# Cross-attention and a top-2 mixture of experts on one core: routing logits from folded weights, norms after the gather, a new lead-in and drain

## What is computed

```python
x = x + xattn(k=ctx, q=layernorm(x), v=ctx)     # 16 heads of 8, causal, out-projection Wo, bias bo
xf = layernorm(x).reshape(1792, 128)
logits = xf @ gate_w + gate_b                   # 8 experts
p, i = top_k(softmax(logits), 2); p = p / sum(p)
# each expert takes its first 280 tokens, in order of the tokens
out = relu(xin @ w1[e] + b1[e]) @ w2[e] + b2[e] # 128 -> 512 -> 128, per expert
x = x + (sum over the token's two experts of p * out)
```

## Time and profile before

| what | value |
|---|---|
| three runs | 191.65, 193.49, 194.66 us (median 193.49) |
| the profiled execution | 194.35 us, of which its span is 192.6 us |
| mean granted TensorE clock | 0.885 |
| busy share of the span: PE, PE weight loads, DVE, ACT, POOL | 83%, 57%, 58%, 45%, 47% |

### The profile page before, as it was taken

The page is one execution under the profiler, slowest core; times in us unless marked ns, Lnnn a source line. Parts: engine busy times, 40 slices in busy tenths (PEclk is TensorE's granted clock), DMA queues, the critical chain, the costliest instruction groups (busy, mean ns, idle before and its releaser), DMA issues.

```text
span 192.6 us, 4628 instructions
## 1 busy us (share of the span) xinstructions
PE 159.1 (83%) x1647; PEld 109.8 (57%) x1651; DVE 110.9 (58%) x395; ACT 87.3 (45%) x196; POOL 90.7 (47%) x152
## 2 busy tenths in 40 slices
PE   6588779999999999999999896965399999998000
PEld 2323537777777777767677543422179988886000
DVE  4666534668889888889886553200026554555064
ACT  3547595979797977884735101000123222330000
POOL 4345290014157765757577787761002644656300
PEclk9855766999999999999999999996859999999655
DMA  5910798995000000000100000003700110111666
GB/s 164 327 75 0 300 388 230 338 311 162 0 3 26 31 29 26 14 27 5 37 0 23 4 20 6 16 8 77 198 0 0 44 39 27 31 34 35 240 189 247
DMA packets 10109, 17.96 MB, mean 93 GB/s; under 512 B 1708, under 2 KB 5568, under 8 KB 9576
## 3 DMA queue, kind: packets, MB, share of 16 engines
q1 hardware_dynamic: 6992, 13.58, 21.4%
q0 software_dynamic: 1632, 2.27, 3.9%
q10 hardware_dynamic: 1464, 1.84, 3.0%
HBM read 11.00 MB, written 7.86 MB: 98 GB/s over the span
## 4 chain that ended last, share of the span: by engine, by line
PE 64%; DMA 8%; POOL 7%; issue 6%; ACT 6%; DVE 5%; ACTq 1%; POOLq 1%; DVEq 1%; SPq 0%
PE score_p L977 10%; PE bank L1005 8%; PE bank L1149 7%; PE bank L992 6%; PE score_p L946 5%; PE score_p L1133 5%; PE bank L1133 5%; POOL slots_d L405 3%; PE bank L905 3%; PE bank L938 3%; DMA chosen<-choice_d 3%; DMA xr<-slots_d 2%; PE bank L1022 2%; PE bank L918 2%; DMA choice_d<-rest_ow,rest_i 2%
## 5 line engine op out<-in xcount | busy, mean ns | idle before, releaser
L405 POOL DMA_INDIRECT slots_d<-rec,slot_i x32 | 32.3, 1008 | 13.9 <-issue 12.4
L911 PE MATMUL score_p<-warm 128*128 128x512 bf16 x91 | 24.9, 419 | 6.0 <-DMA slots_d<-rec,slot_i 3.8
L443 POOL DMA_INDIRECT choice_d<-ow,dst_i x16 | 16.0, 1000 | 29.3 <-DVE ow L871 26.4
L674 DVE TENSOR_REDUCE row_max<-score_p 128x16 f32<-128x912 f32 x16 | 17.7, 1104 | 10.6 <-PE score_p L977 10.6
L977 PE MATMUL score_p<-head_keys,queries 32*32 32x228 f32 (+1 forms) x384 | 22.1, 409 | 0.0
L550 ACT ACTIVATE probsT<-bank 128x512 f32<-128x512 f32 x32 | 18.2, 600 | 5.0 <-PE bank L992 4.9
L992 PE MATMUL bank<-ident,probs 128*128 128x128 f32 x128 | 19.6, 291 | 0.0
L911 PEld LDWEIGHTS score_p<-warm 128*128 128x128 bf16 x95 | 9.5, 106 | 16.9 <-DMA slots_d<-rec,slot_i 4.3
L677 DVE TENSOR_TENSOR probs<-score_p,row_max 128x912 f32<-128x912 f32 x16 | 17.7, 1109 | 1.6
L335 POOL TENSOR_TENSOR rs<-ve,minus_half 128x2 f32<-128x2 f32 x8 | 6.3, 791 | 24.8 <-DVE ve L653 21.2
L1005 PE MATMUL bank<-vals,probsT 128*64 128x18 f32 x512 | 17.8, 212 | 0.0
(11 more groups left out here) (130 smaller groups left out, 281.7 us busy)
## 6 DMA issues: line engine op xcount, KB each, us to landing
choice_d<-chosen SPq DMA_DIRECT2D x2, 1024.0 KB, 8.1
w_s<-w_in SPq DMA_DIRECT2D x1, 2048.0 KB, 8.9
slots_d<-zeros SPq DMA_DIRECT2D x1, 1242.0 KB, 4.4
xg<-slots_d SPq DMA_DIRECT2D x8, 138.0 KB, 4.1
chosen<-choice_d SPq DMA_DIRECT2D x1, 1024.0 KB, 5.0
xs<-x_in SPq DMA_DIRECT2D x1, 768.0 KB, 7.1
ctxT<-ctx_t_in SPq DMA_DIRECT2D x1, 768.0 KB, 8.4
b_s<-b_in SPq DMA_DIRECT2D x1, 512.0 KB, 9.0
```

Source lines behind the costliest of these rows:

```text
L405: gp.indirect_dma_start(out=slots_d, out_offset=bass.IndirectOffsetOnAxis(ap=slot_i[t % 2][:, k, p:p + 1], axis=0), in_=rec[t % RECS][:, p ...
L443: gp.indirect_dma_start(out=choice_d, out_offset=bass.IndirectOffsetOnAxis(ap=where, axis=0), in_=rows, in_offset=None, bounds_check=N_DST ...
L674: ve.reduce_max(row_max[:, p, :], heads, X).then_inc(max_d, 1)
L911: mm(bank[0], warm[:, 0:128], warm[:], start=True, stop=True)
```

## The change

1. **Logits.** A layer norm is linear but for its mean and its factor rs, so logits = rs * ((x + attention + bo) @ G) + gate_b with G = the gate weights less their column means. `centre_gate` makes G (`gate_c`) once on TensorE, `fold_gate` makes Wo @ G once and puts it beside Wo. `output` then multiplies `yT` by 136 columns in place of 128 and adds `xT` (x transposed, given by the host, bo added on GpSimd by `add_bo_T`) times G, 8 columns. `turn_moe`, `empty_moe` and `gate` go. VectorE copies the 16 raw logits out (`gates`) and multiplies by rs in `choose` (two instructions in place of one).
2. **Records.** `x2` now lies inside the record, which also holds mean and rs; `records` goes, and so do the three buffers with their waits. The rows are normalised after the gather: `normalise_slots(e)` and `normalise_rest`, two VectorE instructions of 128x128 for each expert and two for the rest, ahead of the transposes.
3. **Order.** The loop runs to step 7 only; what followed is written out. `choose` is for group g-2 in step g (behind `softmax(2g+1)`), `ranks` and `slots` for g-3 stand earlier in the step. Norm and projection run one group ahead in place of two. The last group's weights are made on VectorE (`weigh_last`).
4. **Lead-in.** The first keys go to a bank of their own, their first copy stands ahead of `empty_norm(0)`, the first queries are copied out on VectorE, 10 filler matmuls stand in the gaps of TensorE, `scores(1)` stands ahead of the wait for the mean, and the clearing of `chosen` on GpSimd comes later.
5. **Gather.** SP issues the load of half of `xr` right behind `xg[0]`; the transposes no longer wait for the third, small one.

```diff
-WARM_START, WARM_TURN, WARM_GATE, WARM_RANK = 11, (2, 4, 12), 2, (4, 6, 8)
-WARM_LAST, WARM_SCATTER, WARM_LANDING = 5, 28, 9
+WARM_LEAD = (3, 2, 2, 3)
+WARM_START = 11
+WARM_MIX, WARM_Y, WARM_CHOICE, WARM_SCATTER, WARM_LANDING = 2, 2, (3, 11), 30, 9
...
+            sp.dma_start(xT[:], x_t).then_inc(xT_in, 16)
...
+                if e == 0:
+                    sp.dma_start(xr[:, 1], by_expert[1]).then_inc(xr_in, 16)
...
             power1(0)
             power1(1)
-            gp.memset(chosen[:, 0], 0.0).then_inc(empties_done, 1)
             means()
...
+            t = GROUPS - 1
+            weigh(t - 2)
+            count(t - 2)
+            scatter(t - 2, 0, 3)
+            power2(t - 1)
+            scatter(t - 2, 3)
+            weigh(t - 1)
+            power2(t)
+            count(t - 1)
+            scatter(t - 1)
+            scatter(t)
...
-            empty_keys("k", 0, 0).then_inc(ring_ev, 1)
+            act.wait_ge(keys0_d, 1)
+            keys0 = probT_b[0][:, 0:2 * GP * S]
+            head_copy(0, 0, keys0)
             empty_norm(0)
-            act.wait_ge(bqs_done, 1)
-            empty_queries("q", 0).then_inc(ring_ev, 1)
+            for h in range(1, SH):
+                last = head_copy(0, h, keys0)
+            last.then_inc(keys0_ev, 1)
...
-            act.dma_start(xr[0:REST, STACKS], by_expert[STACKS - 1, STACK - 1]).then_inc(xr_in, 16)
+            act.dma_start(xr[:, 0], by_expert[0]).then_inc(xr_in, 16)
+            act.dma_start(xr[0:REST, STACKS], by_expert[STACKS - 1, STACK - 1]).then_inc(xr_last_in, 16)
...
-            def records(t):
...
             def choose(t):
...
+                dve.wait_ge(rs2_d, t + 1)
...
                 for p in range(GP):
+                    ve.scalar_tensor_tensor(logits[:, p, :], gates[:, p, :], rec[:, GP * t + p, RS:RS + 1],
+                                            gate_b[:, E * p:E * (p + 1)], mult, add).then_inc(logits_d, 1)
...
+            def normalise_slots(e):
+                dve.wait_ge(xg_in[e], 16)
+                for t in range(FULL):
+                    ve.tensor_scalar(xg[:, e, t, 0:D], xg[:, e, t, 0:D], xg[:, e, t, MEAN:MEAN + 1], xg[:, e, t, RS:RS + 1],
+                                     sub, mult).then_inc(xgn_d, 1)
...
             def expert(e, i):
+                if e + 1 < E:
+                    normalise_slots(e + 1)
...
             def output(t):
+
+                pe.wait_ge(xboT_d, t + 1)
                 pe.wait_ge(ring_ev, filled("y", t))
                 to = take_post("wo", t)
...
+                    n = GP * t + p
+                    mm(to[:, WO * p:WO * (p + 1)], yT[:, 128 * p:128 * (p + 1)], wvo_s[:, D:D + WO], start=True, stop=False,
+                       skip_group_check=True)
+                    last = mm(to[:, WO * p + D:WO * (p + 1)], xT[:, 128 * n:128 * (n + 1)], gate_c[:], start=False, stop=True,
+                              skip_group_check=True)
...
+            keep_warm(WARM_LEAD[2], probT_b[1][:])
             project(1)
+            keep_warm(WARM_LEAD[3], probT_b[1][:])
+            scores(1)
             pe.wait_ge(mean_done, 1)
             tr(post("mean", 0)[:, 0:B], mean[:], ident[0:B, 0:B]).then_inc(post_d, 1)
-            scores(1)
-            values(0)
+            centre_gate()
             transpose_probs(0)
             transpose_probs(1)
-            norm(2)
-            project(2)
...
             def transpose_slots(e, i):
-                pe.wait_ge(xg_in[e], 16)
+                pe.wait_ge(xgn_d, FULL * (e + 1))
```

More of the change, by code:

```diff
@@ new lines, in statistics2, with choose @@
+            def statistics2(t):
+                dve.wait_ge(x2_d, t + 1)
+                hold(dve, passed["dve"])
+                tiles = slice(GP * t, GP * (t + 1))
+                stats(x2[:, tiles, :], stat2, rec[:, tiles, MEAN:RS + 1], stat2_d, mv2_d, GP * t)
+                wait(dve, rs2_d, t)
+                ve.tensor_scalar(ve2[:], rec[:, tiles, RS], 1e-5, None, add).then_inc(ve2_d, 1)
+            def choose(t):
+                tiles = slice(GP * t, GP * (t + 1))
+                dve.wait_ge(rs2_d, t + 1)
+                dve.wait_ge(post_read, posted("wo", t))
+                wait(dve, top_i_d, t)
@@ L784, in _ @@
             statistics1(1)
+            dve.wait_ge(ring_d, filled("q", 0))
+            ve.tensor_scalar(queries[0][:], ring("q", 0)[:, 0:GT], SCALE, bqs[:], mult, add).then_inc(ring_ev, 1)
+            shift1(1)
             keep(slice(GP, PAIRS), 2)
@@ L794, in _ @@
             statistics1(2)
+            softmax(1)
             shift1(2)
@@ new lines, in _ @@
+                if g >= 2:
+                    statistics2(g - 2)
+                softmax(GP * g + 1)
+                if g >= 2:
+                    choose(g - 2)
+                if 0 <= g + 3 < GROUPS:
+                    statistics1(g + 3)
+                divide(GP * (g - 1))
+            t = GROUPS - 1
+            divide(PAIRS - 3)
+            slots(t - 2)
+            divide(PAIRS - 2)
+            residual(t - 1)
+            statistics2(t - 1)
+            divide(PAIRS - 1)
+            choose(t - 1)
@@ new lines, in _, with normalise_rest @@
+            residual(t)
+            statistics2(t)
+            slots(t - 1)
+            choose(t)
+            weigh_last(t)
+            slots(t)
+            def normalise_slots(e):
[3 more added lines that the diff above has]
+                                     sub, mult).then_inc(xgn_d, 1)
+            def normalise_rest():
+                dve.wait_ge(xr_in, 16 * STACKS)
+                for k in range(STACKS):
+                    ve.tensor_scalar(xr[:, k, 0:D], xr[:, k, 0:D], xr[:, k, MEAN:MEAN + 1], xr[:, k, RS:RS + 1], sub, mult)\
+                        .then_inc(xrn_d, 1)
@@ L874, in expert @@
                     weigh_rest(2, slice(0, REST), 3)
+            normalise_slots(0)
+            normalise_rest()
             dve.wait_ge(wb_in, 32)
@@ L1097, in _ @@
                 transpose_probs(4 * g + 1)
+            t = GROUPS - 1
+            mix(PAIRS - 3)
+            ranks(t - 2)
+            mix(PAIRS - 2)
+            turn_y(t - 1)
+            transpose_probs(UNITS - 2)
+            transpose_probs(UNITS - 1)
+            output(t - 1)
+            mix(PAIRS - 1)
+            keep_warm(WARM_MIX)
+            turn_y(t)
+            keep_warm(WARM_Y)
+            output(t)
+            keep_warm(WARM_CHOICE[0])
+            ranks(t - 1)
+            keep_warm(WARM_CHOICE[1])
+            ranks(t)
             def transpose_slots(e, i):
-                pe.wait_ge(xg_in[e], 16)
+                pe.wait_ge(xgn_d, FULL * (e + 1))
                 wait(pe, xgT_ev, e - 1)
```

399 lines of the change are left out of this document (200 added, 199 removed).

## The result

The changed kernel took 180.31, 180.39, 184.67 and 184.69 us, median 182.53; the kernel before took 191.65 to 194.66, median 193.25, on the same chip. The forecast was 178.0 with a range of 173 to 184. The profiled execution of the changed kernel took 180.31 with a span of 178.6; that of before took 194.35 with a span of 192.6. So -14.0 between the two traces, where the forecast was -16.6.

What follows compares the result with a forecast made beforehand. TensorE was taken to bound the loop steps and experts, GpSimd to pace the drain. -9.7 - 0.8 - 2.5 - 2.3 - 1.8 + 0.5 = -16.6 gave 177.75 for an execution like the profiled one, forecast as 178.0, range 173 to 184.

Steps and rivals of the forecast that it cites:

- The lead-in: Stretch up to the heads of step 2: these start at 29.0 in place of 38.69, so -9.7 us.
- The rival with the fallen clock: Lead-in: the clock falls all the same and costs 4 us more, giving 182; chance 15%.
- the 0 that was taken: Lead-in: cost of GpSimd's clearing of `chosen` holding VectorE, taken as 0 of 0 to +1.8 us.
- The steps: Loop steps 2 to 6: 51.35 us in place of 52.15, so -0.8, bounds -1.2 and +2.4.
- near 10.35: Steps 3 to 6: VectorE's time per step after losing `records` and gaining a copy and a small instruction, taken as step time.
- TensorE's own 10.27: Loop steps: TensorE's time per full step, from 10.64, losing record transposes and gate and gaining two products.
- The rival named for this: Steps are VectorE's: the residual waits for `output`, 0.8 a step, making 11.1 a step and 181.5 us; chance 5%.
- The drain: Step 7's heads to the last record's landing, paced by GpSimd: 38.75 us in place of 41.2, so -2.5.
- The gather: Last record's landing to first w1 matmul: 5.3 us in place of 7.6, so -2.3.
- landed 3.2 us behind the records: Gather: both halves of `xr`, moved ahead in their queues, land 3.2 us after the records.
- The clock behind the gather: First expert: fillers and less idle time recover clock loss, -1.8 us of 0 to -2.6.
- Expert 1: Added normalisations on VectorE not hidden there, with `set_rest` in front: +0.5 us, range 0 to +1.

Runs made afterwards that it cites:

- run 1: Changed kernel without the ten filler matmuls of the lead-in: 180.68, 185.61, 186.01 and 186.04 us.
- run 3: Changed kernel without the two products of the input with the centred gate in each output stage: 179.4 us, one execution.
- run 4: Changed kernel with two normalisations of a record put back on VectorE behind choose in each step, into an unread tile: 184.18 us.
- run 10: Changed kernel with epsilon added to both variances on GpSimd, not VectorE; on another chip: 208.88 us, beside 211.09 to 215.69 for the kernel before.
- run 12: Changed kernel with the four edits of run 11, and epsilon on GpSimd up to group 5; another chip: median 202.07 us, kernel before 211.23.
- run 6: Changed kernel with group 6's power behind two scatters, not three, and set_rest inside expert 1: 181.95 us.
- run 5: Changed kernel with SyncE waiting for both halves of xr before loading xg 1 to 7: median 180.66 us, ratio 0.9423.
- run 7: Changed kernel with seven and two filler matmuls in the two holes of the gather: 178.63 us, one execution.
- run 9: Changed kernel with xr's second half issued ahead of xg[0]; another chip: 205.37 us, beside 211.09 to 215.69 for the kernel before.
- run 11: Changed kernel with the edits of run 6 and run 7 plus four fillers ahead of pair 2's scores; another chip: 198.83 to 203.11 us, ratio 0.939.

## Why the prediction was right, and where it was wrong

The forecast of 178.0 lies 2.3 below the shortest execution (180.31) and 4.5 below the median, within the range of 173 to 184.

**The lead-in (-9.7, came -9.8)** holds in place and size: heads of pair 2 at 18.95 (said 18.7), of step 2 at 28.88 (said 29.0), VectorE's small instruction behind the mask down from 1.32 to 0.20. But the reason given for the clock was the order, which "leaves no idle stretch over 1 us". It leaves one of 1.09, and without the ten fillers, which the prediction's working doesn't count, three of four executions were long and the profiled one lost 5.9 of the 9.8 (run 1). So that the term came out whole in the profiled execution is in part luck. The rival with the fallen clock, put at 15% and +4, happened in four of nine profiled executions with this lead-in (1.5 to 2.9 late), and two of the changed kernel's four executions were 4.4 longer for a reason that no trace shows.

The clearing of `chosen` (18.42 to 20.23) met VectorE's small instruction at 19.38, which took 0.87 and ended with it, against 0.17 otherwise. The prediction had named this from the Trainium skill, SBUF — State Buffer, section "The single rule", by which one of the two engines holds the shared ports for its whole instruction; this row agrees. The softmax behind it started 0.19 behind the end of its scores, where it is 0.11 otherwise, so the 0 that was taken stands within 0.1.

**The steps (-0.8, came +0.5).** Two terms failed. "9.95 for step 2" was 10.46: it was 10.10 before, when TensorE had no records to transpose and no gate in it to lose, and it gains the products (run 3 takes 0.34 off it). And "near 10.35" for steps 3 to 6 was 10.72, 10.70, 10.52 and 10.26. The 10.35 was VectorE's term, reckoned from less work than before, and that is where it went wrong: VectorE was busy for 9.65, 9.55 and 9.45 in steps 3 to 5, where it had been for 9.23, 9.50 and 8.88. The prediction counted on TensorE the norm and projection that the old lead-in had done ahead, and not the statistics that VectorE makes for them: six such instructions on `xs` lie in steps 3 to 5, where it was two. Runs 3 and 4 show that VectorE sets steps 3 to 5, where what is taken off TensorE brings nothing. TensorE's own 10.27 isn't borne out either: with VectorE relieved, step 3 stays at 10.48 (runs 10 and 12). The rival named for this had the right engine and the wrong price (0.8 a step through the wait for `output`; steps 3 to 5 came out 0.2 to 0.4 above 10.35), and 5% was too little for it.

**The drain (-2.5, came -3.1)** was GpSimd's, as said. The scatters of group 5 began to be paid for at 95.19, 13.65 behind the heads of step 7 (said 14.0), and from there to the last scatter's end it took 23.3 (said 23.6). What wasn't foreseen is the 0.67 us that GpSimd waits for the choice of group 6, whose power stands behind three scatters; run 6 took it out. The sign "a granted clock of 1.00 from about 5 us to the landing" failed here: it was 0.50 from 96 to 100 us. No run fills that hole, so what it costs isn't known.

**The gather (-2.3, came -1.4).** The step that failed is "landed 3.2 us behind the records": xr came 4.5 behind them. From issue to landing the half on SP's queue takes 4.08 now, and the load waited for before took 4.48; what was gained is mostly that the load the transposes wait for is issued 0.45 behind the landing and not 1.87, minus 0.6 for the normalising. Run 5 shows that the loads behind it in the queue aren't the reason; what is, stays open. The Trainium skill, DMA: Bandwidth & Descriptors, section "Issuing engines are not separate DMA queues", gives an issue on another queue no more than the time of the issue. This trace agrees in part, since 1.42 of the 1.82 by which `xr` landed earlier is time of issue. By the one issue (0.5) that the prediction drew from it the gather would have come to -0.5, as far from -1.4 on the one side as the forecast on the other.

**The clock behind the gather (-1.8, came -0.95)** was mis-sized: the first expert took 5.70 in place of 6.65. Thirty fillers ahead of the landing and nine right at it don't help against the 4 us behind them (122 to 126) in which TensorE works for 1.04; "no such hole behind it" is what failed. Nine more fillers in those 4 us gave another 1.68 (run 7): together the 2.6 that was the far end of the term. **Expert 1 (+0.5)** came out at +0.64, and run 6 showed that `set_rest` is its cause.

So the direction and the place of nearly every gain were right. The sum was 2.6 too good: 1.3 in the steps, 0.9 in the gather, 0.85 in the clock and some 0.2 in small things (0.14 of it at expert 1), less 0.6 that the drain gave more.

## What to carry to other kernels

An engine that is busy for all of a step isn't thereby its bound: here TensorE and VectorE were level within some 0.3 us (step 3 took 10.72, and 10.48 once VectorE was relieved), and only two runs, one taking work off the one and one putting work on the other, told which of them set which step. Work that an order moves out of a lead-in has to be counted on every engine that does a part of it. Where a stretch of waiting can't be removed, fill it on TensorE right up to the work that follows: nine filler matmuls inside the gather were worth 1.7 us, while thirty-nine ahead of it were not enough. And an instruction that starts a chain of choices must not stand behind slow scatters in its engine's queue: moving one power ahead of one scatter took out 0.66.

## What was not expected of the hardware

- Kernels with the same lead-in had their clock fallen or not from one execution to the next: heads of step 2 at 28.88 in some and 30.38 to 31.77 in others, and one kernel, without fillers, took 180.68 beside 185.6 to 186.0.
- On two chips all kernels were slower by a tenth (before: 212.87 and 211.23 against 193), and all four traces taken there have holes in TensorE's stream of short matmuls, from 51 to 54 us on (at the heads in runs 9 and 11, at others in runs 10 and 12), behind which the clock was at 0.50. Why the instructions come late there stays open.
- The load of half of `xr`, 70 KB, takes 4.1 us from issue to landing where `xg[0]`, with 140 KB, takes some 2.2, though both read single records; the rows of `xr` lie in four runs of 32. Issued ahead of `xg[0]` in the same queue it holds it up to 4.4 (run 9, one execution; 2.3 on the same chip in the old order). Why it is slower stays open.
